# The opening of a four-layer chain: LoRA factor B in two transfers, a delta block in the wait for B3, the codebook on another queue

## The reference

```
x = x + (x @ W0.T + b0) + coeff[b] * (x @ (2*mask[b]-1))        # layer 0
delta = (lora_B @ lora_A) * 0.5                                  # 1024 x 1024, rank 64
q  = nearest level of codebook/max|codebook| for (W1+delta)/exp(scale_log)
x = x + x @ (q*exp(scale_log) + delta).T                         # layer 1
x = x + x @ W2.T + b2 + 2 * (x @ A2[slot2[b]]) @ B2[slot2[b]]    # layer 2
x = x + (x @ B3[slot3[b]].T) @ A3[slot3[b]].T                    # layer 3
```

## Time and profile before

| | |
|---|---|
| median of three runs | 560.57 us (560.44 to 560.99) |
| the profiled execution's own time | 559.99 us |
| its span, first to last instruction | 557.9 us |
| PE busy | 542.8 us, 97% |
| DVE busy | 398.8 us, 71% |
| ACT busy | 332.1 us, 60% |
| POOL busy | 151.2 us, 27% |
| HBM traffic | 143 GB/s over the span |

### The profile page before, as it was taken

One profiled execution on the slowest core, in us unless ns is written; L12 is line 12 of the kernel. 1 busy time (PEld: TensorE's weight loads), 2 busy tenths in 40 slices (PEclk: granted clock), 3 DMA queues, 4 the chain that ended last, 5 costly groups with the idle time before them and its releaser, 6 DMA issues.

```text
span 557.9 us, 8879 instructions
## 1 busy us (share of the span) xinstructions
PE 542.8 (97%) x2892; PEld 463.5 (83%) x2892; DVE 398.8 (71%) x624; ACT 332.1 (60%) x624; POOL 151.2 (27%) x166
## 2 busy tenths in 40 slices
PE   4999999999998999999999999999999999999997
PEld 4988888888887788888888888888888888888886
DVE  5998898998857876685775867658477676856631
ACT  3777767767647765574566565557456556654720
POOL 2769778987700040021011002102100300210200
PEclk9999999999999999999999999999999999999999
DMA  8766042732776983491483367249038435814201
GB/s 229 248 86 141 21 151 82 230 106 92 145 212 203 270 247 108 138 243 40 141 198 114 132 153 204 69 157 244 37 132 192 146 130 134 224 40 151 74 0 75
DMA packets 138120, 80.07 MB, mean 144 GB/s; under 512 B 95664, under 2 KB 111024, under 8 KB 138096
## 3 DMA queue, kind: packets, MB, share of 16 engines
q1 hardware_dynamic: 137520, 78.71, 50.6%
q0 software_dynamic: 288, 1.05, 0.5%
q10 hardware_dynamic: 288, 0.01, 0.0%
HBM read 65.59 MB, written 14.16 MB: 143 GB/s over the span
## 4 chain that ended last, share of the span: by engine, by line
PE 84%; DVE 8%; ACT 3%; DMA 3%; issue 1%; POOL 0%; DVEq 0%; ACTq 0%; SPq 0%; POOLq 0%
PE bank L1410 20%; PE bank L1440 10%; PE bank L1439 10%; PE bank L1441 10%; PE bank L1411 10%; PE bank L1304 5%; PE bank L1306 5%; PE bank L1305 5%; PE bank L1452 3%; PE bank L1214 2%; PE bank L1459 1%; DVE w_lo L982 1%; ACT bank L567 1%; PE bank L1228 1%; DMA mask_ring<-in_mask_Bx4096x_ik 1%; ACT pooled L556 1%
## 5 line engine op out<-in xcount | busy, mean ns | idle before, releaser
L1410 PE MATMUL bank<-x_t_pair,m_hi 128*128 128x512 f32 x512 | 181.7, 399 | 2.5 <-DVE m_lo L1082 2.5
L1411 PE MATMUL bank<-x_t_pair,m_lo 128*128 128x256 f32 x512 | 143.8, 281 | 0.0
L733 ACT CAST m_hi<-merged_ring 128x512 fp32r<-128x512 f32 x128 | 76.6, 620 | 78.7 <-DVE merged_ring L1076 39.4
L1410 PEld LDWEIGHTS bank<-x_t_pair,m_hi 128*128 128x128 f32 x512 | 96.2, 188 | 27.2 <-DVE m_lo L1082 3.3
L1082 DVE TENSOR_TENSOR m_lo<-merged_ring,m_hi 128x512 fp32r<-128x512 f32 x128 | 84.4, 687 | 32.8 <-ACT m_hi L733 32.6
L532 POOL TENSOR_TENSOR x_t_pair<-x_sum,x_t_pair 128x256 fp32r<-128x256 f32 x32 | 24.7, 800 | 284.1 <-ACT x_t_pair L778 284.1
L1439 PE MATMUL bank<-P_hi,x_t_pair 128*128 128x512 f32 x256 | 99.7, 389 | 0.0
L1440 PE MATMUL bank<-P_lo,x_t_pair 128*128 128x512 f32 x256 | 99.7, 389 | 0.0
L1441 PE MATMUL bank<-P_hi,x_t_pair 128*128 128x512 f32 x256 | 99.6, 389 | 0.0
L1411 PEld LDWEIGHTS bank<-x_t_pair,m_lo 128*128 128x128 f32 x512 | 96.7, 189 | 0.3
L1076 DVE TENSOR_TENSOR merged_ring<-merged_ring,w_t 128x1024 f32<-128x1024 f32 x64 | 77.6, 1221 | 18.9 <-ACT merged_ring L723 17.0
(11 more groups left out here) (151 smaller groups left out, 862.1 us busy)
## 6 DMA issues: line engine op xcount, KB each, us to landing
mask_ring<-in_mask_Bx4096x_ik SPq DMA_DIRECT2D x64, 512.0 KB, 4.9
out<-out_staged SPq DMA_DIRECT2D x32, 256.0 KB, 2.0
w_nat<-in_L_cond_W SPq DMA_DIRECT2D x14, 512.0 KB, 4.8
x_squares<-in_x SPq DMA_DIRECT2D x56, 128.0 KB, 3.0
w_raw<-in_L_cond_weight SPq DMA_DIRECT2D x16, 256.0 KB
g_batch<-g_dram SPq DMA_DIRECT2D x32, 128.0 KB, 3.0
w0t_dram<-w_out SPq DMA_DIRECT2D x14, 256.0 KB, 2.7
w_t<-w0t_dram SPq DMA_DIRECT2D x6, 512.0 KB, 5.0
```

Of the source, the lines that this page charges most:

```text
L733: nc.scalar.copy(Mh[:, n % MR], ring_f[:, k % MR, h * HALF:(h + 1) * HALF]).then_inc(s["h_set"], 1)
L1410: mm(full, mh, xThl[:, k].rearrange("p i t -> p (i t)"), start=(k == 0), stop=False, skip_group_check=True)
L1411: ins = mm(full[:, 0:T], ml, xTh[:, k], start=False, stop=(k == KT - 1), skip_group_check=True)
```

## The change

Five edits, all in the opening. Factor B of LoRA is loaded in two transfers of 128 KB, each with a semaphore of its own, and PE waits for the half that it transposes next. `delta(0)` waits only for the first half of `lbt`, `delta(1)` for the second. `delta(2)` moves from after `v_part(4)` to directly after `w2_transpose(0)`, ahead of the wait for B3. The codebook's transfer leaves SP's queue and becomes the third that ACT issues. Nothing else differs, and every line from there on stands one to three lines lower.

```
-            sp.dma_start(lbn[:, :, :], lora_b.rearrange("(t p) r -> p t r", p=P)).then_inc(s["lora_b_in"], 16)
+            lora_b_rows = lora_b.rearrange("(h t p) r -> h p t r", h=2, p=P)
+            for h in range(2):
+                sp.dma_start(lbn[:, h * HT:(h + 1) * HT, :], lora_b_rows[h]).then_inc(lora_b_in[h], 16)
             sp.dma_start(la[0:RL, :], lora_a).then_inc(s["lora_a_in"], 16)
-            sp.dma_start(cb[:, :], row(codebook).broadcast_to([P, NCB])).then_inc(s["cb_in"], 16)
...
                 act.dma_start(tok[:, i], v.rearrange("(o n) -> o n", o=1).broadcast_to([P, NB])).then_inc(s["tok_in"], 16)
+            act.dma_start(cb[:, :], codebook.rearrange("(o n) -> o n", o=1).broadcast_to([P, NCB])).then_inc(s["cb_in"], 16)
...
-            pe.wait_ge(s["lora_b_in"], 16)
             for h in range(2):
+                pe.wait_ge(lora_b_in[h], 16)
...
-                elif n == 0:
-                    pe.wait_ge(s["lbt_set"], 2)
+                elif n < 2:
+                    pe.wait_ge(s["lbt_set"], n + 1)
...
             w2_transpose(0)
+            delta(2)
             b3_transpose(0)
...
             v_part(4)
-            delta(2)
             w2_transpose(5)
```

More of the change, by code:

```diff
@@ L198, in cond_resid_chain @@
         NORM = 6
-        s = {n: sem(n) for n in """cb_in sc_in late_in lora_b_in lora_a_in w1_in0 w1_in1 a2_in b2_in a3_in b3_in w0_in w0_in2 w0_out_st0 w0_out_st1 g_stored y_stored
+        s = {n: sem(n) for n in """cb_in sc_in late_in lora_b_in0 lora_b_in1 lora_a_in w1_in0 w1_in1 a2_in b2_in a3_in b3_in w0_in w0_in2 w0_out_st0 w0_out_st1 g_stored y_stored
             ub_in b2row_in x_in0 x_in1 g_in recip_set first_level tok_in b2c_in b2col_set numbers_set rows_set ident_set ident_zero own_a own_b own_set ub_zero
@@ L211, in cond_resid_chain @@
         x_in = [s["x_in0"], s["x_in1"]]
+        lora_b_in = [s["lora_b_in0"], s["lora_b_in1"]]
         out_stored = [s["out_st0"], s["out_st1"]]
```

## The result

The changed kernel took 561.46 us in the median of 11 runs (560.72 to 563.20), beside 560.57 for the kernel before (560.0 to 561.0, 11 runs). The ratio is 1.0022, 95% interval 1.0014 to 1.0029. So it is slower, by 0.9 us in the medians and 1.2 us by the ratio, where 0.15 us less was forecast. The 11 runs lie in two groups, 560.7 to 561.5 and 562.4 to 563.2. The profiled execution, with 562.41 us and a span of 560.4, belongs to the upper one. Five of the first 11 runs lay above 561.9 us, and two of the 12 there. How much slower it is therefore varies with the session. Why it can be slower, the traces show.

A forecast was written before the change was run, and what follows sets the result against it. PE is busy 97%, but a chain over DVE, ACT and POOL bounds the opening (12 to 56 us). Only 0.15 us was to reach the end: median 560.57 to 560.4 us, no measurable change, range 559.6 to 561.2.

The forecast's parts named there:

- B3 landing: Opening: B3 still lands at about 14.3 us; change taken as 0, bounds -0.4 to +0.4 us.
- Rival 1: Opening: B3 lands earlier and the chain moves with it, gaining up to 0.5 us, to 560.1 us; 18%.
- PE's pace: PE in the wait for B3: delta(2) takes 0.89 us and fits into the 1.39 us wait.
- `delta(0)`: PE's opening: starts at 7.3 to 7.8 us instead of 8.32, when factor A lands; PE 0.5 to 1.0 us earlier there.
- The first comparison: DVE's opening: comparisons of half 0 start 0.35 to 0.6 us earlier than before.
- the codebook: DVE's wait at 7.56 us: issuing the codebook from ACT gains 0 to 0.63 us there, taken as 0.5.
- The wait at the sixth block near 32 us: PE at 32.10 us: its wait for DVE's w_lo grows from 0.53 to 1.27 us.
- `delta(2)` by itself: PE: moving delta(2) only turns 0.89 us of idle time at B3 into idle time at 32 us, worth nothing.
- The 0.15 us over POOL: DVE's identity block near 26.5 us ends with POOL's sum, so term_c's 0.15 us gain passes on to the end.
- B3's `w_hi`: ACT at 16.03 us: two w_hi follow B3's landing and limit DVE's gain of 0.35 to 0.6 us to 0.15.
- The fourth rival: Opening: factor A lands late, so delta(2) ahead of B3 makes PE late; slower, for example 561.7 us; 5%.
- the rest of the chain: From 32.10 us over DVE, POOL and ACT to P_lo at 56.64: no late transfer, so 0.15 us reach the end.

The follow-up runs named there:

- e5: Changed kernel, with POOL also waiting for factor A to land before it issues B3; ratio 1.0002 to the kernel before.
- e1: Changed kernel with delta(2) back at its old place after v_part(4); ratio 1.0015 to the kernel before.
- e13: Changed kernel, B3 held until the codebook landed, second block of W2 held until the first half block of W1 landed; ratio 1.0001 to the kernel before.
- e2: Kernel before with only delta(2) moved ahead of the wait for B3; ratio 1.0003 to the kernel before.
- e3: Kernel before with only the codebook's transfer moved to ACT's queue; ratio 1.0002 to the kernel before.
- e9: Kernel before with delta(2) moved and the second block of W2 held until the first half block of W1 landed; ratio 0.9997 to the kernel before.
- e12: The changed kernel unaltered, measured and profiled a second time; ratio 1.0005 to the kernel before, profiled execution 561.19 us.
- e4: Kernel before with only factor B in two transfers and the split waits; ratio 1.0021 to the kernel before.
- e10: Changed kernel, factor A issued between factor B's halves, delta(2) ahead of w2_transpose(0), second block of W2 held for W1's first half block; ratio 1.0004 to before.
- e7: Changed kernel with B3 held until factor A landed and delta(2) back at its old place; ratio 1.0016 to the kernel before, median 562.23 us.

## Why the prediction was wrong

The failing step is one sentence: "It was issued at 7.22 by POOL, released by the tokens, which the change leaves alone." The change does not touch the tokens' transfers, but they land with SP's first one, and that became half as long. In the sum this is the term "B3 landing", set to 0 with bounds of -0.4 to +0.4 us. It measured -2.1 us (12.2 against 14.3), and it cost time. Three things followed or came on top:
- **B3** was issued at 5.72 and landed at 12.2 (5.72 + 6.5). Rival 1 had it early and counted that as a gain. It asked what an earlier B3 releases, and not whom it delays. The windows of before and of after show the load (columns: window, length, PE busy, granted clock, share of the transfer engines, GB/s):

```profile
10.00:12.00 2.00, 2.00 (x11) 1.00 1.01 401
```

```profile
10.00:12.00 2.00, 1.71 (x9) 1.00 1.01 408
```

  The total rate is about the same. What it carries is not: from 8 to 12 us the queue of POOL's indirect transfer moved 0.07 MB in the kernel before and all 0.52 MB of B3 in the changed one (columns: packets, MB, share of 16 engines):

```profile
q0 software_dynamic: 17, 0.07, 4.4%
```

```profile
q0 software_dynamic: 144, 0.52, 34.4%
```

  So the first block of W2 comes later. The Trainium skill, DMA: Bandwidth & Descriptors, section "Issuing engines are not separate DMA queues", says that transfers run on the same 16 transfer engines and interleave, whichever engine started them. This case's traces agree with the sharing. The e5 run, where B3 alone was held, puts a number on it: W2 was used at 11.12 instead of 12.52, so 1.40 of the 1.90 us of lateness are B3's in these profiles. (In e1, with the same transfers in the same order, W2 was used at 11.78, so the size varies.) The other 0.50 us stayed with B3 out of the way, in e5 as in e13, and are not explained; without the halves W2 was used at 10.45 to 11.00 (e2, e3, e9).
- **The first block of W2** was in no term. DVE's `w_lo` for it stands among the comparisons, so its lateness counts, with 0.78 us at `P_lo` by e12.
- **PE's pace** at `delta(2)` was taken from the earlier trace rows at 27.85, where it is full. The sum used 0.89 us, and it took 1.71 (14.78 to 16.49), with `w2_transpose(0)` another 0.9 us longer. The earlier trace rows had both paces: 3.75 us for sixteen at 8.32 and 1.06 for eight. That is the other 1.19 us of the profile. This share does not follow from B3 being early: the same program with B3 just as early ran at full pace in e12.

Of the other steps: `delta(0)` at 7.96 against 7.3 to 7.8, bound by factor A, as said, with all of its delay. The first comparison moved by 0.33 us against 0.35 to 0.6; the codebook was in early (6.31), but the scales were next and held DVE until 8.50, which was not in the sum. The wait at the sixth block near 32 us grew to 0.94, where 1.27 was said: by e2 and e9, DVE's fixed distance between two blocks sets it. That `delta(2)` by itself is worth nothing was right (e2). The 0.15 us over POOL rests on DVE's instruction ending with POOL's sum; all 14 traces agree, with DVE's end 0.15 to 0.17 us behind POOL's. But e9 shows that B3's `w_hi` did not bind as tightly as claimed: it came 1 us earlier and gained 0.06. The fourth rival, the one for the slower side, came nearest: PE was late at B3 with `delta(2)` ahead. But its trigger was factor A, it had 5%, e4 lost as much without `delta(2)` there, and 1.68 us of DVE's 2.02 us of waiting lay at the first block of W2, ahead of B3. That the rest of the chain carried the delay on to `P_lo` was right.

## What to carry to other kernels

When a transfer at the start is made shorter, list every other transfer whose landing shifts with it, then what those landings release, and whose bytes that pushes back; an earlier prefetch is a loss if it overtakes the operand that is needed first. In an in-order pipeline, work put into a wait is free at the trace's arrival times only; check it with the awaited data as much earlier as the change can make them (2.1 us here), and at PE's lower pace. And if gates lie within half a microsecond of each other, moving one gains what separates it from the next: in e13, 0.13 of 0.38 us reached `P_lo`.

## What was not expected of the hardware

- The tokens' two small transfers, issued by ACT at 0.8 and 1.3 us, were used 0.11 to 0.35 us behind SP's first transfer in every trace, whether that was 256 KB of factor B (PE at 5.67, tokens at 5.87), 128 KB of it (4.11 and 4.37), or factor A (landed at 5.6, tokens at 5.88). In e10, with factor A behind the first half, both came later together (4.70 and 4.81). Why is open.
- PE's pace in the opening differs between executions of one program. In one profile of the changed kernel the clock rose to 2.4 GHz at 11.09 us, ahead of a 1.5 us gap, and stayed there; in the other it rose at 16.58, 3.5 us behind a 1.3 us gap. That is 1.19 us of 560, with the tokens, B3, the first block of W2 and DVE's first comparison within 0.05 us of each other. After a rise, the only fall in the openings was that of e7: behind 2.15 us of idleness, to 1.2 GHz for 3.4 us.
- An indirect transfer issued at 7.2 us landed after 7.1 us when two more blocks of W2 stood in SP's queue, and after 4.7 us when these were held back and issued at 8.3 and 8.7 us (e9).
